# Two-layer hybrid block on one core: turned-block copies on ScalarE, first causal heads beside a feed-forward, paired fan of the inverted sums

## What is computed

```
def _L0_attn_b_ref(x, w_qkv, b_qkv, w_out, b_out):      # 16 heads of 16
    qkv = x @ w_qkv + b_qkv
    ...
    dot = jnp.einsum('bhid,bhjd->bhij', q, k)
    q_norm_sq = jnp.sum(q * q, axis=-1, keepdims=True)
    k_norm_sq = jnp.sum(k * k, axis=-1, keepdims=True)
    vals = q_norm_sq + k_norm_sq.transpose(0, 1, 3, 2)
    scores = dot * dot / (vals - 2.0 * dot + EPSILON) * SCORE_SCALE
    mask = jnp.triu(jnp.ones((Lq, Lq), dtype=scores.dtype), k=1) * -1000000000.0
    attn = jax.nn.softmax(scores + mask[None, None, :, :], axis=-1)
    out = jnp.einsum('bhij,bhjd->bhid', attn, v)
    ...
    return out @ w_out + b_out

# feed-forward of the layer f
    h = (h - mu) / jnp.sqrt(var + 1e-05) * lg + lb
    h = h @ w1 + b1
    a, g = jnp.split(h, 2, axis=-1)
    h = a * jax.nn.gelu(g, approximate=False)
    x = x + h @ w2 + b2
```

## Time and profile before

| | us |
|---|---|
| median of 3 runs | 4490.21 |
| lowest and highest of them | 4489.77, 4497.48 |
| the profiled execution's own time | 4488.74 |
| its span, first to last instruction | 4486.5 |

### The profile page before, as it was taken

The page is one execution under the profiler, slowest core; times in us unless marked ns, Lnnn a source line. Parts: engine busy times, 40 slices in busy tenths (PEclk is TensorE's granted clock), DMA queues, the critical chain, the costliest instruction groups (busy, mean ns, idle before and its releaser), DMA issues.

```text
span 4486.5 us, 65884 instructions
## 1 busy us (share of the span) xinstructions
PE 4149.7 (92%) x23120; PEld 2608.4 (58%) x23120; DVE 3315.1 (74%) x7977; ACT 2541.7 (57%) x5478; POOL 1658.1 (37%) x1816
## 2 busy tenths in 40 slices
PE   8999989999999999988888887888999999999997
PEld 5666556566566566555555555554566665665664
DVE  5667777777667667559999999998677776677662
ACT  4555554454454454439888888876454454454441
POOL 1222365445446456330000010013464464465541
PEclk9999999999999999987888889888999999999998
DMA  2000000000010000000000000101000000100000
GB/s 75 10 16 6 24 10 6 3 3 6 23 29 12 11 8 11 23 21 20 20 22 20 20 23 22 34 20 34 3 6 3 3 25 8 34 15 17 15 17 21
DMA packets 63095, 78.33 MB, mean 17 GB/s; under 512 B 15344, under 2 KB 47520, under 8 KB 62768
## 3 DMA queue, kind: packets, MB, share of 16 engines
q1 hardware_dynamic: 62768, 74.12, 5.8%
HBM read 36.37 MB, written 12.58 MB: 11 GB/s over the span
## 4 chain that ended last, share of the span: by engine, by line
PE 63%; DVE 23%; issue 6%; ACT 4%; POOL 2%; DMA 0%; SPq 0%; POOLq 0%; DVEq 0%; ACTq 0%
PE wide L823 43%; PE o_ps L823 7%; PE wide L826 6%; PE turn_ps L826 4%; DVE x L1246 3%; DVE turned L1297 2%; DVE w_up L1359 2%; PE turn_ps L823 2%; DVE prob L1371 2%; DVE x L1365 2%; DVE prob L1382 2%; DVE w_up L1344 1%; POOL prob L1575 1%; DVE turned L1283 1%; DVE hid L1365 1%
## 5 line engine op out<-in xcount | busy, mean ns | idle before, releaser
L823 PE MATMUL wide<-x,w_up 128*128 128x512 f32 (+5 forms) x2560 | 856.6, 552 | 5.5 <-DVE x L1463 4.1
L823 PE MATMUL wide<-w_in,x_t 128*128 128x512 f32 (+2 forms) x1920 | 811.7, 566 | 15.8 <-ACT q_t L1122 8.3
L1575 POOL TENSOR_SCALAR prob<-prob,st 128x256 f32<-128x256 f32 (+1 forms) x1024 | 496.3, 503 | 821.7 <-DVE st L1395 819.1
L1182 ACT ACTIVATE prob<-prob,st 128x256 f32<-128x256 f32 (+1 forms) x1024 | 479.2, 471 | 251.5 <-DVE st L1382 251.2
L823 PEld LDWEIGHTS wide<-w_in,x_t 128*128 128x128 f32 x1920 | 341.4, 192 | 368.6 <-issue 359.0
L823 PEld LDWEIGHTS wide<-x,w_up 128*128 128x128 f32 (+2 forms) x2560 | 377.2, 198 | 291.9 <-issue 279.3
L823 PE MATMUL o_ps<-pt,v 128*32 128x128 f32 (+2 forms) x5120 | 509.3, 345 | 16.8 <-DVE pt L1411 5.4
L1548 POOL TENSOR_TENSOR sines<-raw,rot 128x512 f32<-128x512 f32 x256 | 351.4, 1393 | 336.7 <-ACT raw L1110 336.4
L1556 POOL TENSOR_TENSOR rn<-ss,minus_half 128x16 f32<-128x16 f32 x128 | 423.1, 3305 | 103.3 <-DVE ss L1292 96.3
L823 PEld LDWEIGHTS o_ps<-pt,v 128*64 128x64 f32 (+1 forms) x5120 | 326.8, 133 | 227.1 <-issue 143.4
L1213 ACT ACTIVATE o_t<-o_ps 128x512 f32<-128x512 f32 x192 | 114.4, 596 | 521.2 <-PE o_ps L823 521.0
(11 more groups left out here) (153 smaller groups left out, 7490.1 us busy)
## 6 DMA issues: line engine op xcount, KB each, us to landing
kept<-resid SPq DMA_DIRECT2D x16, 512.0 KB, 3.0
x<-kept SPq DMA_DIRECT2D x16, 512.0 KB, 3.3
w_up<-hid SPq DMA_DIRECT2D x64, 128.0 KB, 2.2
x<-hid SPq DMA_DIRECT2D x64, 128.0 KB, 2.4
shifted<-resid SPq DMA_DIRECT2D x32, 224.0 KB
w_in<-in_f_wqkv SPq DMA_DIRECT2D x4, 1536.0 KB, 6.3
w_up<-in_f_w SPq DMA_DIRECT2D x4, 1492.0 KB, 6.7
resid<-in_x SPq DMA_DIRECT2D x8, 512.0 KB, 8.9
```

The costliest lines, as they stand in the source:

```text
L823: return eng.matmul(out, lhsT, rhs, start=start, stop=stop, skip_group_check=True)
L1182: last = eng.activation(pr[:, local_span(t)], pr[:, local_span(t)], ACT.Exp, bias=sm[:, t:t + 1], scale=-1.0, accum_out=sm[:, 4 + t:5 + t])
L1575: last = eng.tensor_scalar(pr[:, local_span(t)], pr[:, local_span(t)], sm[:, 8 + t:9 + t], 1.0, ALU.mult, ALU.mult)
```

## The change

Three edits, and a new plan of all queues from unit 23 on.

1. `pt_b` keeps the masked blocks alone. The two plain blocks of each third step become a part `pt_c` on ACT, queued behind `pt_b` (so that the two engines never read that bank together); `mix` and the next user of the pair wait for it too.
2. `fan` and `out_b` go from four parts to two. One fan makes two head groups into a `wide` pair, one `out_b` multiplies 1024 columns; `fan` is no longer in `NARROW`, the parts held in `turn_ps`.
3. The first three steps of unit 24 may run before unit 23's feed-forward ends. Their rows lie in `sines` (`early_rows`), their denominators and inverses in `prob2` and `prob3`, and they use the two others as `prob`. Each of them lets the one ahead end its `bmul` first (`close_free`). The feed-forward parts of unit 23 get earlier due times (`after`).

```diff
+FIRST_B = [stage for stage, _ in PLAN].index("b") * SEQS
+def early(u, k):
+    return u == FIRST_B and k < 3
+def early_group(u, k):
+    return u == FIRST_B and k < 6
...
+        if early(u, k):
+            n_prob = 2
...
+    if kind == "pt_c":
+        return 0.3
...
-                    put(kind + "_c", g, at - 4 / steps, final(kind, g), ("bdot", *free), ("down", u - 1, 3))
+                    put(kind + "_c", g, at - 4 / steps, final(kind, g), ("bdot", *free),
+                        ("join" if early_group(u, k) else "down", u - 1, 3))
...
+            ffn = [] if early(u, k) else [("down", u - 1, 3), ("up_h", u - 1, 2), ("back", u - 1, 0)]
...
+            if early(u, k):
+                three = (u, k - 1)
+                ffn = [("turn_a", u - 1, STEPS["f"] - 1), ("turn_b", u - 1, STEPS["f"] - 1)]
+            put("bclip", k, at, final("bdot", k), ("bmul", *three), *ffn)
+            put("bnum", k, at, final("bdot", k), *turned, ("bmul", FIRST_B, 2) if u == FIRST_B and k >= 3 else None)
...
+            if k % 3 == 2:
+                put("pt_c", k, at + 2 / steps, final("pt_b", k), *mixed)
...
-        for g in range(PAIRS):
+        for g in range(2):
             put("fan", g, u + 1, final("osum"))
             put("out_b", g, u + 1, final("fan", g))
...
+    after = lambda late: u + .9 if u == FIRST_B - 1 else u + 1 + late
...
-NARROW = ("bk", "bq", "turn_a", "turn_b", "sel", "fan")
+NARROW = ("bk", "bq", "turn_a", "turn_b", "sel")
...
+        early_rows = [sines[0][:, 0:512], sines[0][:, 512:1024], sines[1][:, 0:512], sines[1][:, 512:1024]]
+        def rows_home(u, g):
+            return early_rows if early_group(u, 6 * g) else [q_rows[g % 2], k_rows[g % 2], q_half, k_half]
+        def close_home(u, i):
+            pair = [prob["prob2"], prob["prob3"]] if early(u, i) else [a[(nth("bguess", u, i) - 1) % 3] for a in (b_den, b_inv)]
+            return [a[:, 0:2 * b_width(i)] for a in pair]
+        def close_free(gate, u, i):
+            if early(u, i):
+                gate.wait_ge(S["bmul"], nth("bmul", u, i) - 1)
+                gate.wait_ge(S["turn_a"], nth("turn_a", u - 1, STEPS["f"] - 1))
+                gate.wait_ge(S["turn_b"], nth("turn_b", u - 1, STEPS["f"] - 1))
...
-                    mm(turn_ps[:, :], sum_fan[:, i, :], b_weight, True, True).then_inc(S["fan"], 1)
+                    for k in range(2):
+                        last = mm(ps[:, 512 * k:512 * k + 512], sum_fan[:, 2 * i + k, :], b_weight, True, True)
+                    last.then_inc(S["fan"], 1)
...
+                elif kind == "pt_c":
+                    act.wait_ge(S["pt_b"], nth("pt_b", u, i))
+                    met, n = P * B_OWN[i % 3], P * len(B_TURNS[i % 3][1])
+                    eng.activation(prob_t[SLOTS[u, i]["pt"]][:, 512 + met:512 + n],
+                                   wide[PLACE["turn_b", u, i]][:, 512 + met:512 + n], ACT.Copy).then_inc(S["pt_c"], 1)
...
-                        if n > met:
-                            last = eng.tensor_copy(pt[:, 512 + met:512 + n], ps[:, 512 + met:512 + n])
...
-                    eng.tensor_tensor(o_t[:, i, :], turn_ps[:, :], o_t[:, i, :], ALU.mult).then_inc(S["out_b"], 1)
+                    pair = o_t[:, 2 * i:2 * i + 2, :].rearrange("p g n -> p (g n)")
+                    eng.tensor_tensor(pair, wide[PLACE["fan", u, i]][:, :], pair, ALU.mult).then_inc(S["out_b"], 1)
```

More of the change, by code:

```diff
@@ L369, in parts_of @@
     for i in range(TILES):
-        put("proj", i, u + 1, final("out_b" if st == "b" else "out", PAIRS - 1),
+        put("proj", i, u + 1, *([final("out_b", 1)] if st == "b" else [final("out", PAIRS - 1)]),
             ("load_out", n * SEQS, 0), ("fold_o_c", 0, 0))
@@ L384, in parts_of @@
+    put("nrm_f", 0, after(0), final("rstd_f"), ("bmul", u - 1, BSTEPS - 1), ("xt2", u - 1, 0), ("back", u - 1, 0))
+    put("bias", 0, after(.2), final("nrm_f"), ("load_up", n * SEQS, 0))
+    put("xt2", 0, after(.2), final("nrm_f"))
+    put("xt2_c", 0, after(.2), final("xt2"), ("up_h", u - 1, 2), ("load_up", n * SEQS, 0))
     for i in range(len(UP_G)):
-        put("up_g", i, u + 1.2 + .12 * i, final("xt2_c"))
-        put("gate", i, u + 1.2 + .12 * i, final("up_g", i), ("down", u - 1, 3), ("bden", u - 1, BSTEPS - 1), ("bdot", u - 1, BSTEPS - 1),
-            ("bmul", u - 1, BSTEPS - 1), ("out_b", u - 1, PAIRS - 1))
@@ L573 @@
         "load_fold fold_q fold_q_c fold_o fold_o_c aq aq_c lat ak_c av_c bqkv row bsq bv bss brow bk bk_c bq bq_c bias_b "
-        "score bden bdot low inv exp wt wt_b bclip bnum bln bguess bclose binv bmul turn_a turn_b neg pt_a pt_b mix sel fan out olog oexp osum out_b load_sel "
+        "score bden bdot low inv exp wt wt_b bclip bnum bln bguess bclose binv bmul turn_a turn_b neg pt_a pt_b pt_c mix sel fan out olog oexp osum out_b load_sel "
         "proj res moved bn_f bn_f2 var_f rstd_f nrm_f bias xt2 xt2_c up_g gate gelu up_h hid down res2 back_in back store "
```

114 lines of the change are left out of this document (60 added, 54 removed).

## The result

The changed kernel took **4505.3 us** (median of 7 runs, 4498.07 to 4510.92) against 4490.69 us for the kernel before (7 runs, 4485.97 to 4497.48). The ratio is 1.0031, 95% interval 1.002 to 1.0042: slower by 14 us, where 17 us faster were predicted. The profiled execution took 4505.3 us, that of before 4488.74.

The account below looks back on a forecast made before the run. DVE was taken to set stage b's pace, ACT not far behind, with PE bounding the stages around it. The terms -10.1 - 7.0 - 5.0 + 5.0 = -17.1 us took 4490.2 to 4473.1 us, range 4454 to 4489.

Parts of the forecast that it names:

- What bounds the kernel: Stage b: DVE, busy 129.2 of 137.2 us a unit, sets the pace; what leaves its queue there counts.
- Plain copies: Stage b: moving 64 copies from DVE to ACT saves 18.5 us, less 8.4 for handing over; net -10.1 us.
- The hand-over: At `pt_c`: ACT's queue and the later-freed wide pair cost 0.15 us a copy, 56 copies, 8.4 us.
- Paired fans: At `out_b`: two fans instead of four save 0.2 us of work and 0.8 of waits a unit, -7.0 us.
- The only rival for it: Fans' waits reappear at `bden`, leaving 0.2 us a unit; part of the eaten-gain rival, 4488.8 us, chance 0.20.
- First heads: First seam, units 23 and 24: early steps beside the feed-forward give -5.0 us, bounds +5 and -8.
- late heads: First seam: step 0 reaches ACT late and holds the Gelu, costing 5 us; 4483.1 us, chance 0.12.
- The end: End of stage b: unit 33's two matmul groups move behind unit 31's `proj`, handing back +5.0 us, bounds 0 to 7.4.
- The slower one, ACT's queue: Stage b: `pt_c` stands at ACT awaiting DVE's product, delaying squares or inverse; 0.8 us a copy, 4509.5 us, chance 0.13.
- The open case: No new wait at `pt_c`, no waits at `out_b`, full 8 us at first seam, nothing handed back; 4441.3 us, chance 0.10.
- the gain is eaten inside the units: Stage b: handing over costs 0.33 us a copy, fans' waits reappear at `bden`, seams cancel; 4488.8 us, chance 0.20.

Follow-up runs that it names:

- e10: Kernel before in its own order, the 64 plain copies on DVE left out (those blocks not filled): 4481.14 us, ratio 0.9968.
- e12: Kernel before in its own order, each plain copy on DVE preceded by a second of the same shape into a spare tile: 4506.7 us, ratio 1.0026.
- e16: Kernel before in its own order, with 64 added ACT copies to a spare tile that nobody waits for: 4508.93 us, ratio 1.0037.
- e1: Kernel before with only the plain copies moved to ACT, behind DVE's masked product: 4494.7 us, ratio 1.0003.
- e11: e1 in exactly its order, with the 64 ACT copies and the waits for them left out: 4478.85 us, ratio 0.9964 of the kernel before.
- e2: Kernel before with only two paired fans in place of four single ones: 4508.8 us, ratio 1.0036.
- e9: Kernel before with its four single fans each in a wide pair in place of turn_ps: 4511.21 us, ratio 1.0051.
- e3: Kernel before with only the first three steps of unit 24 allowed beside unit 23's feed-forward: 4493.06 us, ratio 1.0000.
- e4: Changed kernel with the plain copies back on DVE, paired fans and first heads kept: 4503.16 us, ratio 1.0025 of the kernel before.
- e14: Kernel before with only the plain copies on ACT, straight after the turned blocks, DVE's masked product behind them: 4485.94 us, ratio 0.9986.
- e15: e14 with the first heads beside the feed-forward too, fans single: 4480.34 us, ratio 0.9974 of the kernel before.
- e5: Changed kernel with its four single fans put back, copies on ACT and first heads kept: 4494.22 us, ratio 1.0007 of the kernel before.
- e7: Kernel before with only paired fans, except in unit 31, which keeps four single fans: 4506.42 us, ratio 1.0035.
- e17: Kernel before with paired fans in unit 31 only, single fans in units 24 to 30: 4487.34 us, ratio 0.9993.

## Why the prediction was wrong, point by point

**What bounds the kernel.** "DVE sets the pace, with ACT not far behind it" was right as an order and wrong as a price. The text then counted each microsecond of DVE in full and each of ACT as free. The runs show 0.68 and 0.55 of DVE's time (14.4 and 11.7 of 21.1 us, e10 and e12) and, as an upper price, 0.84 of ACT's (16.6 of 19.8 us, e16).

**Plain copies** (-10.1 forecast, +1 measured, e1). The gain was -18.5, by e10 it is -14.4. The hand-over was +8.4, by e1 and e11 it is 17.5. Two steps failed. "The work itself is thus hidden under ACT's waits for DVE and PE": it isn't (e16). And 0.15 us a copy was taken "because DVE waited for ACT only once in six units", while 0.27 us was measured. That row told of waits for ACT before ACT had a copy to be late with; the row that bore on it was the other one in the same paragraph, PE's 18.4 us for the end of L1411 (24.0 us over all its rows), and these waits went to 78.2. The own bounds of the term (nothing to 0.33 us) held the measured size.

The copy takes 366 ns on ACT and 412 on DVE, as forecast from the earlier trace rows. The Trainium skill (ScalarE: Activation LUTs, Rules for kernel authors) gives simple elementwise work to VectorE, per element up to about 3 times as fast in bf16. In this case's trace, which is fp32 out of PSUM, the copy is no slower on ScalarE; the move failed for another reason than the rule's.

**Paired fans** (-7.0 forecast, +16 alone, +11 in the changed kernel). This is the step that turned the sign. What was said of the place itself came true in the changed kernel: 16 instructions of 1.224 us, and 11.6 us of waits before them in place of 23.8. The fall of the waits is luck, though: with the fans alone they rose to 28.2 us (e2), and only where the copies had moved too did they fall. What failed is the bound: "all 3.0 us go, or none", which left the term at -1.0 us a unit; in its place single fans in `wide` pairs alone cost 23 us (e9), and paired ones 16. The sentence before it names the cause, that "each takes two of three wide pairs from the steps", and then gives it no price beyond the wait that it was to save. The only rival for it ended at 0.2 us a unit, so no case had the fans on the losing side.

**First heads** (-5.0 forecast, 0 measured, e3, interval -4 to +4). The mechanism ran: DVE is busy 34.5 us in the 50 us up to 2000 (24.9 before, 30 wanted). This execution runs 4.5 us behind that of before already at the residual add of unit 22 (1867.1 against 1862.6), so positions have to be read from there. The Gelu went from 1961.09 to 1966.88, of which 1.3 us are its own where 3 were forecast, with the table loads of 1.28 us beside it:

```profile
1965.58 1.28 ACT L1285 ACT_TABLE_LOAD   x1
1966.88 2.34 ACT L1285 ACTIVATE hid<-hid 128x2560 f32<-128x2560 f32 x1
...
1987.72 1.23 DVE L1550 TENSOR_TENSOR resid<-wide,resid 128x1024 f32<-128x1024 f32 x1 [4.72 <-PE wide L875]
```

PE covered it: from the residual add of unit 22 the second add of 23 comes after 120.6 us, 121.5 before, so that the 1987.7 here is the execution's offset and not late heads. What failed is the step from there to the gain, that 7.3 us on DVE earlier in the chain are 5 us off the time. In e3 the second add of unit 23 comes 3.6 us earlier after that of unit 22 than before, and the residual add of unit 24 doesn't: 286.5 us after that of unit 22 against 286.6. What takes the head start back inside unit 24 was not asked. Together with another part the heads gave -5 (e2 to e4), -5 (e14 to e15) and +2 (e1 to e5), all with intervals that overlap; whether they give anything is not settled beyond that.

**The end** (+5.0 forecast). Units 31 to 33 took 309.9 us against 300.1, +9.8, where up to 7.4 was the bound. The two groups behind `proj` are there, and unit 33 is 4.4 us longer. But in e1, which has the copies without the fans, these units took 297.2 us and unit 33 84.4: this term belonged to the fans, not to a seam that takes back any gain.

**The rivals.** The slower one, ACT's queue, came near the time (4509.5) by a mechanism that isn't there: ACT never stood before `pt_c`, and its waits for DVE fell from 43.4 to 25.4 us. The open case was backed by "DVE is never late for ACT", which the rows contradict: ACT waited 43.4 us for DVE's row maxima; it was DVE that hardly waited for ACT. In the copies alone "the gain is eaten inside the units" is what happened.

## What to carry to other kernels

Where three engines pass each step on to one another, idle time on one isn't room: price each microsecond moved by a run that adds it and one that takes it away (here 0.55 to 0.68 us on VectorE, up to 0.84 on ScalarE). When work is handed to another engine, look at who waits for the last reader of its buffer, and try which of the two engines should read last: the same copy, put before the masked product in place of behind it, made the difference between no gain and a gain. And a scarce buffer has a price of its own: a saving that takes two of three rooms must be costed by everything that wants them, not by the wait that it removes.

## What the runs showed of the hardware

The same instructions in the same order don't take the same time, and the granted clock of PE goes along with it. Units 7 and 8, before and then changed, with equal code:

```profile
521.00:609.50 88.50, 81.84 (x451) 48.54 (x450) 64.42 (x125) 45.50 (x101) 40.08 (x33) 1.00 0.02 7
609.50:679.00 69.50, 59.77 (x315) 38.20 (x314) 51.80 (x129) 36.36 (x94) 48.19 (x48) 0.95 0.05 16
```

```profile
520.30:611.80 91.50, 85.01 (x452) 50.10 (x450) 64.40 (x125) 45.53 (x101) 40.12 (x33) 0.96 0.02 7
611.80:683.30 71.50, 61.76 (x314) 38.99 (x313) 51.80 (x128) 36.37 (x94) 48.27 (x48) 0.93 0.04 16
```

5 us of the 16.9 between the two profiles arise here, at a granted clock of 0.96 and 0.93 in place of 1.00 and 0.95, and part of it is gone again by the end. In stage b it is the same: units 25 to 30 are planned alike in e2 and e7, and took 834.5 us at a granted clock of 0.87 (PE busy 675) and 840.9 at 0.85 (PE busy 692):

```profile
2148.77:2983.32 834.55, 675.39 (x5116) 425.40 (x5117) 766.83 (x1745) 700.81 (x1241) 76.20 (x106) 0.87 0.09 22
```

```profile
2149.20:2990.07 840.87, 691.79 (x5116) 434.52 (x5117) 767.56 (x1745) 701.33 (x1242) 76.10 (x106) 0.85 0.08 22
```

DVE is as busy in both, so the longer stretch goes with PE's clock and not with DVE's work. That fits with DVE's time being worth only a part of itself, but PE's share wasn't measured by a run of its own.

The same holds for the runs, and it leaves a rival for the price of the copies. The runs of the kernel before that were taken beside e14 to e17 go from 4479.24 us at a mean granted clock of 0.957 to 4503.16 us at 0.950. The twelve runs of e1 go from 4481.06 us at 0.954 to 4506.75 us at 0.945, those of e5 from 4477.61 us at 0.955 to 4502.58 us at 0.946: 13 of these 24 runs have a lower clock than any run of the kernel before, while e14 stays between 0.951 and 0.956. At 0.953 and 0.954 the three runs of e1 took 4481 to 4485 us, the four of e14 at 0.954 took 4483 to 4486 us, and the nine of the kernel before beside e1 took 4489 to 4498 us. So what the late copy costs goes together with a lower clock; by these few runs it costs nothing at the same clock. Whether the late copy lowers the clock and the clock costs the time, or the longer waits merely show as a lower mean, no run here separates. For the paired fans it is otherwise: e2 took 4502 to 4508 us at 0.955, where the kernel before took 4486 to 4493 us at 0.955 and 0.956.
